# A conditioned transformer block on one core: GpSimd's weight preparation without its hold, its source buffer reloaded earlier

## The reference

```python
def rmsnorm(x, w): return x * rsqrt(mean(x * x, -1) + 1e-6) * w
def film(x, cond, w, b):
    scale, shift = split(cond @ w + b, 2)
    return x * (1 + scale) + shift
h = film(rmsnorm(x, norm1_w), cond, film1_w, film1_b)
Q, K, V = h @ q_w + q_b, h @ k_w + k_b, h @ v_w + v_b
x = x + softmax(Q @ K.T * 512 ** -0.5) @ V @ proj_w + proj_b
h = film(rmsnorm(x, norm2_w), cond, film2_w, film2_b)
x = x + gelu(h @ mlp_w1 + mlp_b1) @ mlp_w2 + mlp_b2        # 2048 hidden features
```

## Time and profile before

| what | value |
|---|---|
| median of 3 runs | 1741.45 us |
| the profiled execution's own time | 1742.31 us |
| its span | 1740.5 us |
| PE busy | 1730.9 us (99%), 8176 matmuls |
| DVE / ACT / POOL busy | 1335.5 / 930.0 / 211.8 us |
| PE clock granted, mean | 0.999 |

### The profile page before, as it was taken

How to read it: one execution, slowest core, us unless ns; L and a number is a source line. 1 busy time by engine, 2 the same in 40 slices (tenths; PEclk the granted TensorE clock), 3 DMA queues, 4 the chain that set the end, 5 groups by cost and what they waited for, 6 DMA issues and landing times.

```text
span 1740.5 us, 23211 instructions
## 1 busy us (share of the span) xinstructions
PE 1730.9 (99%) x8176; PEld 1452.7 (83%) x8176; DVE 1335.5 (77%) x1907; ACT 930.0 (53%) x1601; POOL 211.8 (12%) x204
## 2 busy tenths in 40 slices
PE   9999999999999999999999999999999999999999
PEld 8888888788888888888888888888888888888887
DVE  6988999777776886697688669758876885885477
ACT  6656565665644654554465445546544554653344
POOL 1468687000000000000000000000000000000000
PEclk9999999999999999999999999999999999999999
DMA  9468687733246678677767877776787777677675
GB/s 359 134 231 312 235 321 270 282 111 91 79 160 209 190 266 267 208 237 262 235 194 266 265 205 233 264 238 193 264 268 205 232 264 240 190 242 244 193 233 200
DMA packets 201859, 395.57 MB, mean 227 GB/s; under 512 B 23888, under 2 KB 27984, under 8 KB 199696
## 3 DMA queue, kind: packets, MB, share of 16 engines
q1 hardware_dynamic: 201488, 393.55, 68.8%
q0 software_dynamic: 112, 0.26, 0.0%
q10 hardware_dynamic: 144, 0.26, 0.0%
HBM read 330.99 MB, written 62.98 MB: 226 GB/s over the span
## 4 chain that ended last, share of the span: by engine, by line
PE 83%; POOL 7%; DVE 3%; DMA 2%; ACT 2%; issue 0%; SPq 0%; POOLq 0%; DVEq 0%; ACTq 0%
PE psum L755 35%; PE psum L775 23%; PE psum L783 12%; PE psum L611 6%; POOL w_out L575 3%; PE psum L725 2%; POOL w_out L573 2%; ACT h L920 1%; DMA w_src<-w_dram 1%; PE psum L660 1%; PE psum L661 1%; PE psum L665 1%; DMA f2w_sb<-f2w_dram 1%; DVE pT_sb L1261 1%; PE psum L675 1%; PE psum L676 1%
## 5 line engine op out<-in xcount | busy, mean ns | idle before, releaser
L755 PE MATMUL psum<-op_hi_P,ring 128*128 128x512 f32 x1792 | 551.6, 389 | 0.0
L775 PE MATMUL psum<-stage_hi,ring 128*128 128x512 f32 x1784 | 440.5, 389 | 0.0
L755 PEld LDWEIGHTS psum<-op_hi_P,ring 128*128 128x128 f32 x1792 | 336.3, 188 | 69.5
L775 PEld LDWEIGHTS psum<-stage_hi,ring 128*128 128x128 f32 x1784 | 334.9, 188 | 69.4
L1007 ACT CAST stage_hi<-x 128x1024 fp32r<-128x1024 f32 x224 | 235.4, 1054 | 235.2 <-PE psum L775 222.8
L755 PE MATMUL psum<-op_lo_P,ring 128*128 128x512 f32 x896 | 348.6, 389 | 0.0
L1473 DVE TENSOR_TENSOR stage_lo<-x,stage_hi 128x1024 fp32r<-128x1024 f32 x224 | 273.5, 1224 | 72.4 <-ACT stage_hi L1007 72.1
L991 ACT ACTIVATE x<-x,vecs 128x512 f32<-128x512 f32 x192 | 138.1, 723 | 278.2 <-DVE x L1460 278.2
L783 PE MATMUL psum<-stage_lo,ring 128*128 128x512 f32 x892 | 238.4, 389 | 0.0
L755 PEld LDWEIGHTS psum<-op_lo_P,ring 128*128 128x128 f32 x896 | 168.2, 188 | 35.0
L783 PEld LDWEIGHTS psum<-stage_lo,ring 128*128 128x128 f32 x892 | 167.5, 188 | 34.7
(11 more groups left out here) (194 smaller groups left out, 2387.3 us busy)
## 6 DMA issues: line engine op xcount, KB each, us to landing
ring<-wu_scratch SPq DMA_DIRECT2D x448, 256.0 KB, 2.9
ring<-wd_scratch SPq DMA_DIRECT2D x448, 256.0 KB, 2.9
x_tok<-x_dram SPq DMA_DIRECT2D x16, 1024.0 KB, 11.6
xT_in<-xT_dram SPq DMA_DIRECT2D x16, 1024.0 KB, 8.4
x2T_scratch<-xT_in SPq DMA_DIRECT2D x32, 512.0 KB, 5.2
hn<-x2T_scratch SPq DMA_DIRECT2D x32, 512.0 KB, 5.3
xres<-x2T_scratch SPq DMA_DIRECT2D x32, 512.0 KB, 4.9
out_dram<-xres SPq DMA_DIRECT2D x31, 512.0 KB, 4.3
```

Source lines behind the costliest of these rows:

```text
L755: mm = pe.matmul(to, wt, b, start=q in FRESH and t == 0, stop=t == len(steps) - 1, skip_group_check=True)
L775: mm = pe.matmul(bank(q, dt), a[:, dt, part, :], stage_hi[r][:, e, :], start=q in FRESH and ss == 0 and e == 0 and part == 0, stop=False, ...
```

## The change

It has five parts:
- `load_w_src(c)` for c > 0 waits for the four sums and the first three splits of chunk c - 1 (`w_mixed` 4c, `w_split` 7(c - 1) + 3) instead of all seven splits.
- For n = 8 the last chunk's seven stores are cut in two: four stand ahead of the loads of the norm row and of xT, three behind.
- GpSimd waits for `key_terms` in chunk 0 only.
- PE's wait for `stat_read` in group 11 moves from ahead of `g_pair(12)` to behind `output(11, 0)`.
- ScalarE's `keep_sums` in group 11 moves behind the copies of V's blocks 2 and 3.

```diff
             def load_w_src(c):
                 if c == 0:
                     sp.wait_ge(vp_full, KD)
-                wait_used(sp, w_split, 7 * c)
+                if c > 0:
+                    sp.wait_ge(w_mixed, 4 * c)
+                    sp.wait_ge(w_split, 7 * (c - 1) + 3)
...
-            def store_w_chunk(c):
-                for i, q in enumerate(PREP_ORDER):
-                    u = 7 * c + i
+            def store_w_chunk(c, some):
+                for i in some:
+                    q, u = PREP_ORDER[i], 7 * c + i
                     sp.wait_ge(w_split, u + 1)
...
+                if n == CHUNKS:
+                    store_w_chunk(n - 1, range(4))
                 if n + 2 <= LAST:
...
                     load_xT(n + 2)
-                if 0 < n <= CHUNKS:
-                    store_w_chunk(n - 1)
+                if 0 < n < CHUNKS:
+                    store_w_chunk(n - 1, range(7))
                 if n == CHUNKS:
+                    store_w_chunk(n - 1, range(4, 7))
                     sp.dma_start(f2w_sb[:], f2w.rearrange("(k p) n -> p k n", p=P)).then_inc(loaded["f2w"], 16)
...
                     if n == 0:
                         pool.wait_ge(vp_full, KD)
-                    pool.wait_ge(key_done, (KD + 1) * (n + 2))
+                    if n == 0:
+                        pool.wait_ge(key_done, (KD + 1) * 2)
                     sum_weights(n)
...
                 v_product(n, 3)
-                if n == 11:
-                    pe.wait_ge(stat_read, 2)
...
                 output(n, 0)
                 if n == 10:
                     pe.wait_ge(film_read, 2)
+                if n == 11:
+                    pe.wait_ge(stat_read, 2)
                 for d in range(1, GB):
...
+                keep_v(n, 2)
+                keep_v(n, 3)
                 if n == 11:
                     keep_sums(0, sums_attn)
-                keep_v(n, 2)
-                keep_v(n, 3)
```

## The result

The changed kernel takes 1744.76 us, the median of 20 runs, against 1740.40 us of the kernel before in 20 runs. The ratio is 1.0023, with a 95% interval of 1.0016 to 1.0029: some 4 us slower. Its profiled execution took 1744.50 us with a span of 1742.6.

What follows compares the result with a forecast made beforehand. PE was taken as the bound, at 29.16 us per group, losing 7.96 us to waits. Winning that and losing 9.7 us to VectorE beside GpSimd turned 1742.3 into 1744.0, or 1743.1 as median; range 1735.5 to 1747.3.

Steps and rivals of the forecast that it cites:

- case A: Groups 2 to 7: losses between 4.5 and 11.4 us about cancel the gain, 1738.0 to 1744.9; chance 0.42.
- C: Rival from group 2 on: pauses feed themselves and the clock falls, 14.3 us lost, 1747.8; chance 0.31.
- film2: Group 9, output 9: f2w lands in time, so the wait and slower matmuls go, 4.93 us won.
- The sums: Group 11, output 11: the copies of the sums no longer delay PE, 0.94 us won.
- xT: Groups 3 and 4: xT's load is issued some 10 us earlier, so the wait for the transposes goes, 2.09 us.
- key_terms: VectorE beside GpSimd: five instructions grow from 3.67 us to 8.0 beside sums, 6.75 beside casts and subtractions.
- rival B: Groups 2 to 8: key_terms suffer less and the gain stands, 1736 or 1733.5; chance 0.27 for over 0.2% faster.
- Groups: PE's losses: 2.6 us in group 2, 1.5 in 3, 1.0 in 4, 1.2 each in 5 to 7, none in 8.
- the clock: Behind group 2's pause: the granted clock may fall as in group 9; half of 1.93 us, 1.0, added.
- low_halves: VectorE on GpSimd's sums: about 0.5 us more in group 2 and 0.7 in group 4.
- D: Group 9 rival: the film2 stall stays, 4.93 us more, 1748 with losses; part of C's chance.
- The signs named ahead: GpSimd idle 9 to 15 us behind outputs, outputs 2 to 7 late behind pT_sb, output 9 at 32.8, 11 at 29.6.

Runs made afterwards that it cites:

- experiment 5: Changed kernel with GpSimd's wait on key_terms put back inside each chunk, between roots and fourth split: 1741.62 us, ratio 1.0005 to the kernel before.
- experiment 9: Changed kernel with each GpSimd chunk held until low_halves of the same group are done, instead of key_terms of the next: 1735.16 us, ratio 0.9968.
- experiment 1: Changed kernel with GpSimd's wait on key_terms back in every chunk, everything else kept: 1735.22 us, ratio 0.9968 to the kernel before.
- experiment 2: Kernel before with only GpSimd's hold on key_terms removed, source still reloaded behind all seven splits: 1740.48 us, ratio 1.0004.
- experiment 6: Changed kernel with the hold on key_terms in chunks 0 to 3 and none in 4 to 7: 1740.18 us, ratio 0.9994.
- experiment 3: Kernel before with only the move of the sums' copies and of PE's wait for them: 1739.87 us, ratio 0.9996.
- experiment 7: Changed kernel, hold back in every chunk, f2w in two halves waited for one by one, second ahead of last three stores: 1734.15 us, ratio 0.9958.

## Why the prediction was right in direction and short in size

The forecast was 1743.1 with a range of 1735.5 to 1747.3, 0.42 for a change within 0.2% and 0.31 for slower by more; measured are 1744.76 and a ratio of 1.0023. The mechanism of case A and its place were right, and the result lies at the border to C. Against the base of 1741.45 the forecast was a change of 1.7 us, and 4.4 were measured. That the two times are only 1.7 apart is in part luck: the base, a median of three runs, was 1.05 us above the median of 20.

- **The gains.** film2: 4.93 of 4.93 us won in the trace. The sums: 0.94 won (29.61 instead of 30.55). xT: the 2.09 us of groups 3 and 4 were read from the one profiled execution, and this is **the step that failed**: it took for a standing cost what stood in that execution alone. Three other profiles with the late reload do not have them, and the profiled execution, at 1742.31, was 1.9 us above the median of 20 runs. The prediction noted that it lay 0.86 above the three runs shown and took only that off. Without the xT term its sum is +3.8 us; the medians differ by 4.4, and the ratio of 1.0023 makes 4.0.
- **key_terms.** Taken as 8.0 us in group 2 and 6.75 later; measured are 7.5 and 5.2 to 6.2, so this term was too large in both. L1227 does wait (1.44 us), and rival B fell with it. By the Trainium skill (SBUF — State Buffer, Who interferes with whom) also a `tensor_scalar` in its two-port mode contends. The wait agrees with that; which mode L1227 runs in, no row shows.
- **Groups.** Predicted 2.6, 1.5, 1.0, three times 1.2, 0, and 1.0 for the clock, 9.7 in all; measured 1.81, 2.54, 2.99, 0.86, 1.05, 0.90, 0.13, in all 10.28. The sum holds, and partly by luck, since the parts do not: the pause long enough for the clock came in group 3, not 2. Its cost shows in output 3 and behind it: 1.6 us of group 4's 2.99, when the 1.19 idle are taken off and 0.2 that a late start costs besides (group 2 lost 1.81 with 1.64 idle).
- **low_halves** were in the sum as an addition of 0.5 to 0.7 us. Experiments 5 and 9 show that from group 5 on the work behind ScalarE's start, `low_halves` above all, carries the loss: with clean `key_terms` it stays, with clean `low_halves` it goes. The sum had this too small and `key_terms` too large.
- **C** was right that a pause brings the clock down and wrong that it snowballs: the losses of groups 5 to 7 stay near 0.9 us. **D** fell: `f2w` was in time. The signs named ahead came too: GpSimd idle 9 to 17 us behind output 4, outputs 2 to 7 late and behind `pT_sb`, output 9 at 32.79 and output 11 at 29.61 us.

## What to carry to other kernels

Where VectorE and GpSimd share a stage, ask for each block of two-input instructions on the critical path which of GpSimd's work lies on it, and add the delays up against the slack: here a group had room for slowed `key_terms` with clean `low_halves`, and for `scale_x` and `low_halves` slowed by the splits, but not for `low_halves` on the sums. Before a wait is removed as idle time, look for what else it does: this hold, and the late reload without it, each kept GpSimd in step with the group, and only the removal of both was dear (9.5 us between the changed kernel and experiment 1). And a term read from a single profile is worth checking against another one, above all if that execution lay off the median.

## What the runs showed of the hardware

**VectorE and GpSimd take turns.** GpSimd beside the `key_terms` of group 2 shown above (96.11 to 100.44 us), two sums and a cast:

```profile
95.75 1.45 POOL L565 TENSOR_TENSOR w_sumP<-w_sumP,w_src 128x512 f32<-128x512 f32 x1
97.28 1.60 POOL L567 TENSOR_TENSOR w_sumP<-w_src,w_sumP 128x512 f32<-128x512 f32 x1
98.82 1.08 POOL L578 CAST w_out<-w_src 128x512 fp32r<-128x512 f32 x1
```

One two-input VectorE instruction passes per GpSimd instruction: beside the sums, 1.3 us alone, it takes 1.65 to 1.78 us, beside a cast, 0.6 us alone, 0.99 to 1.1, and alone 0.69 to 0.75. GpSimd's own grow as well, a sum to 1.6 and a cast to 1.08. Even a 128x4 instruction takes 1.2 us beside a sum (0.16 alone, experiment 5). The four of `add_output`, with one input in PSUM, take 2.73 us beside GpSimd as they did before. The length of a GpSimd instruction thus sets the price, and a block of VectorE is hurt most by GpSimd's longest ones.

**The clock does not fall after each pause.** Behind PE's pause of 3.00 us in the earlier trace rows, which ended at 323.24, the granted clock read 0.72 over six microseconds; it read 0.73 behind 2.25 us in the changed kernel, 0.72 behind 2.01 us in experiment 5 and 0.62 behind 3.9 us in experiment 2. But it read 1.00 behind 2.35 us in experiment 6, and behind 3.25 us in experiment 3 (windows of the kernel before, then of experiment 3, where the pause ended at 321.17):

```profile
322.00:328.00 6.00, 4.76 (x14) 3.75 (x15) 3.12 (x14) 6.00 (x17) 0.00 (x0) 0.72 0.56 181
...
322.00:328.00 6.00, 6.00 (x28) 4.97 (x27) 2.51 (x7) 6.00 (x15) 0.00 (x0) 1.00 0.67 218
```

What decides was not found. It fits that kernels with such a pause scatter (the kernel before 1738.8 to 1743.7, the changed one 1740.9 to 1746.2), while the kernel of experiment 7, which has none, stays within 1734.09 and 1734.27 in its five runs; that this is the cause was not tested. What made xT late in the one profile stays open too.
